# A two-stage conv network with four Fourier layers on one core: H transforms by even and odd halves, inverse W transform ahead of the second norm

## The reference, cut to what matters

```python
x = L0(x)                     # 3x3 conv, leaky relu, 1x1 conv to 9 weights, softmax, 9-tap filter per pixel
for j in range(4):            # x: 8 images, 32 channels, 64 x 64, float32
    Kj, Lj = project(K[j]), project(L[j])        # less the mean of the nine taps
    z = relu(batchnorm(conv3x3(x, Kj), gamma[j], beta[j]))      # conv1, first norm
    x = x + 0.1 * conv3x3T(z, Kj)                               # conv2
    x = batchnorm(x, gamma[j], beta[j])                         # second norm
    Bh = fft2(Lj, rolled and padded to 64 x 64)                 # one filter per channel
    t = 1.0 / (0.1 * (Bh.real ** 2 + Bh.imag ** 2) + 1.0)
    x = real(ifft2(fft2(x) * t))
```

## Time and profile before

| | |
|---|---|
| median of 3 runs | 695.11 us (694.95 to 696.44) |
| the profiled execution | 699.56 us, its span 697.7 us |
| TensorE (PE) busy | 643.2 us (92%) |
| VectorE (DVE) busy | 487.7 us (70%) |
| ScalarE (ACT) busy | 355.3 us (51%) |
| GpSimd (POOL) busy | 95.5 us (14%), all in the prologue |
| mean granted TensorE clock | 0.978 of full speed |

### The profile page before, as it was taken

One profiled execution on the slowest core, in us unless ns is written; L12 is line 12 of the kernel. 1 busy time (PEld: TensorE's weight loads), 2 busy tenths in 40 slices (PEclk: granted clock), 3 DMA queues, 4 the chain that ended last, 5 costly groups with the idle time before them and its releaser, 6 DMA issues.

```text
span 697.7 us, 13525 instructions
## 1 busy us (share of the span) xinstructions
PE 643.2 (92%) x5392; PEld 221.3 (32%) x5392; DVE 487.7 (70%) x843; ACT 355.3 (51%) x672; POOL 95.5 (14%) x92
## 2 busy tenths in 40 slices
PE   6597999999999989999999899999998999999982
PEld 4222333222333333233333332333333323333330
DVE  3669888875886794638867946398679453886783
ACT  1454666663796223528961325299523152994233
POOL 0367666672000000000000000000000000000000
PEclk9689999999999999999999999999999999999996
DMA  9995111115800013583000226730003177100044
GB/s 187 183 171 91 32 32 33 31 31 127 190 2 1 1 28 97 131 176 102 1 1 1 52 72 156 155 99 1 1 1 79 46 176 154 40 1 1 1 105 137
DMA packets 44781, 51.10 MB, mean 73 GB/s; under 512 B 36528, under 2 KB 36656, under 8 KB 42672
## 3 DMA queue, kind: packets, MB, share of 16 engines
q1 hardware_dynamic: 40240, 48.95, 32.9%
q10 hardware_dynamic: 4480, 1.30, 1.2%
HBM read 11.96 MB, written 4.19 MB: 23 GB/s over the span
## 4 chain that ended last, share of the span: by engine, by line
PE 77%; DVE 15%; issue 3%; ACT 2%; DMA 1%; SPq 1%; POOL 0%; DVEq 0%; ACTq 0%; POOLq 0%
PE psum L978 48%; PE psum L1050 6%; PE psum L1146 5%; PE psum L1113 5%; PE psum L1129 3%; PE psum L1160 3%; PE psum L1001 3%; DVE work L923 2%; PE psum L1038 2%; DVE spare L895 1%; DVE work L889 1%; ACT Z L614 1%; DVE work L905 1%; DVE work L879 1%; PE psum L1080 1%
## 5 line engine op out<-in xcount | busy, mean ns | idle before, releaser
L978 PE MATMUL psum<-Z,wts 128*32 128x512 f32 x1536 | 168.2, 593 | 6.4 <-DVE Z L846 6.4
L978 PE MATMUL psum<-X,wts 128*32 128x512 f32 x1536 | 170.1, 593 | 0.6 <-issue 0.6
L593 ACT ACTIVATE work<-X,small 128x512 bf16<-128x512 f32 x128 | 90.7, 710 | 48.6 <-DVE X L864 48.6
L768 DVE BATCH_NORM_STATS2 stats<-Z 128x6 f32<-128x512 f32 x60 | 41.3, 692 | 79.3 <-ACT Z L508 79.2
L508 ACT ACTIVATE Z<-psum 128x512 f32<-128x512 f32 x64 | 38.2, 597 | 104.3 <-PE psum L978 93.2
L978 PEld LDWEIGHTS psum<-Z,wts 128*32 128x32 f32 x1536 | 51.6, 109 | 121.5 <-issue 108.5
L978 PEld LDWEIGHTS psum<-X,wts 128*32 128x32 f32 x1536 | 47.9, 109 | 111.7 <-issue 110.7
L571 ACT ACTIVATE Z<-Z,small 128x512 f32<-128x512 f32 (+4 forms) x92 | 80.2, 922 | 5.2 <-DVE small L836 4.7
L864 DVE SCALAR_TENSOR_TENSOR X<-psum,X 128x512 f32<-128x512 f32 x64 | 43.6, 690 | 39.0 <-PE psum L978 38.8
L1146 PE MATMUL psum<-work,cstS 128*128 128x512 f32 x128 | 59.2, 605 | 4.7 <-DVE work L889 3.9
L1129 PE MATMUL psum<-work,cstS 128*128 128x496 f32 x128 | 56.3, 582 | 0.0
(11 more groups left out here) (122 smaller groups left out, 772.7 us busy)
## 6 DMA issues: line engine op xcount, KB each, us to landing
X<-X SPq DMA_DIRECT2D x64, 260.0 KB, 4.0
Z<-Z SPq DMA_DIRECT2D x32, 520.0 KB, 8.0
Z<-x SPq DMA_DIRECT2D x36, 128.0 KB, 4.2
out<-Z SPq DMA_DIRECT2D x24, 128.0 KB, 2.2
parS<-par SPq DMA_DIRECT2D x4, 673.0 KB, 8.6
Z<-x SPq DMA_DIRECT2D x12, 120.0 KB, 5.3
Z<-x ACTq DMA_DIRECT2D x14, 64.0 KB, 4.4
Z<-x SPq DMA_DIRECT2D x14, 64.0 KB, 4.7
```

Of the source, the lines that this page charges most:

```text
L593: nc.scalar.activation(by_row(rest[:, o:o + N // 2].bitcast(bf16)), xc, what, bias=small[:, 26:27], accum_out=sums[:, NCH * i + c:NCH * i ...
L768: nc.vector.bn_stats(stats[:, 6 * c:6 * c + 6], rows(Z0, REG, c // Q, CH * (c % Q), CH))
L978: last = nc.tensor.matmul(out_b[C * r:C * r + C, :], weights[:, o:o + C], rows(src, reg, bp, g, CH, dj - 1), start=(dj == 0), stop=(dj == ...
```

## The change

Four things are done together.

1. **H by halves.** GpSimd's `mix_halves` adds and subtracts image rows h and h + 32 of each pair, from X0 into Z0, as soon as conv2's chunks are there; `turn` reads Z0. The H transform of a sum gives the even and that of a difference the odd frequencies, so fwdH and invH become matmuls of 64 x 64 where there were 128 x 128. Two chunks together are four such matmuls on four quadrants of the array. `unmix_halves` adds and subtracts again after the inverse, from Z0 into X0. In the last layer invH stays a 128 x 128 matmul and gives the rows directly.
2. **Inverse along W ahead of the norm.** invW of pairs 0 and 1 runs before the second norm; `move_back` writes Z0, raw, and ScalarE's `scale_x` (step "affine") scales X0 in place, two operations of 1024 elements per pair (four of 512 before). In the last layer it writes Z2 from Z0.
3. **Order.** The transform steps stand one behind each chunk of conv2; fwdH of pair 3 moves behind conv1's chunk 1. `turn` of a pair stands behind the first conv2 chunk of the next pair, that of pair 3 behind the second norm and `prepare`.
4. Constants for the new matmuls; slot 0 takes seven small matmuls per pair, a table four (now three each, with half the columns or half the outputs).

```diff
     after = {
-        5: fourier(j, 0, "fwdW"),
-        9: fourier(j, 0, "fwdH") + fourier(j, 1, "fwdW"),
-        13: fourier(j, 0, "invH") + fourier(j, 1, "fwdH") + fourier(j, 2, "fwdW"),
-        15: fourier(j, 1, "invH") + fourier(j, 2, "fwdH"),
+        6: fourier(j, 0, "fwdW"),
+        8: fourier(j, 0, "fwdH"),
+        9: fourier(j, 1, "fwdW"),
+        10: fourier(j, 0, "invH"),
+        11: fourier(j, 1, "fwdH"),
+        12: fourier(j, 0, "invW"),
+        13: fourier(j, 2, "fwdW"),
+        14: fourier(j, 1, "invH"),
+        15: fourier(j, 2, "fwdH"),
     }
     for c in range(NCH):
-        steps += [("conv2", j, c), ("turn", j, c)] + after.get(c, [])
-    steps += [("norm", j, 2)] + fourier(j, 3, "fwdW") + fourier(j, 0, "invW") + fourier(j, 2, "invH")
-    steps += fourier(j, 1, "invW") + fourier(j, 3, "fwdH")
-    rest = {1: fourier(j, 3, "invH"), 3: fourier(j, 2, "invW"), 5: fourier(j, 3, "invW")}
+        steps.append(("conv2", j, c))
+        if c and c % Q == 0:
+            steps.append(("turn", j, c // Q - 1))
+        steps += after.get(c, [])
+    steps += [("moments", j)] + fourier(j, 1, "invW") + [("norm", j, 2), ("affine", j, 0), ("turn", j, BP - 1), ("affine", j, 1)]
+    steps += fourier(j, 3, "fwdW") + fourier(j, 2, "invH")
+    rest = {
+        1: fourier(j, 3, "fwdH"),
+        2: fourier(j, 2, "invW"),
+        3: fourier(j, 3, "invH"),
+        5: fourier(j, 3, "invW") + [("affine", j, 2)],
+        9: [("affine", j, 3)],
+    }
...
+            def mix_halves(j, bp, i):
+                bk.result(NUMBER["conv2", j, bp * Q + 2 + i])
+                low, high = (rows(X0, REG, bp, CH * (2 * half + i), CH) for half in range(2))
+                for half, op in enumerate((ALU.add, ALU.subtract)):
+                    nc.gpsimd.tensor_tensor(rows(Z0, REG, bp, CH * (2 * half + i), CH), low, high, op=op)\
+                        .then_inc(halves_mixed, 1)
+
+            def unmix_halves(j, bp):
+                pool.wait_ge(rows_back, 2 * (BP * j + bp) + 2)
+                pool.wait_ge(x_summed, 2 * (NCH * j + Q * bp + Q))
+                even, odd = (rows(Z0, REG, bp, 2 * CH * p, 2 * CH).rearrange("p g (b w) -> p g b w", b=2) for p in range(2))
+                for half, op in enumerate((ALU.add, ALU.subtract)):
+                    dst = rows(X0, REG, bp, 2 * CH * half, 2 * CH).rearrange("p g (w b) -> p g b w", b=2)
+                    nc.gpsimd.tensor_tensor(dst, even, odd, op=op).then_inc(parts_added, 1)
+
+            for j in range(DEPTH):
+                for what, *at in layer_steps(j):
+                    if what == "conv2" and at[1] % Q > 1:
+                        mix_halves(j, at[1] // Q, at[1] % Q - 2)
+                    elif what == "invW" and at[1] % Q == 0 and j + 1 < DEPTH:
+                        unmix_halves(j, at[1] // Q)
...
-            def keep_invW(j, c):
+            def scale_x(j, bp):
...
+                for h in range(2):
+                    if j == DEPTH - 1:
...
+                    else:
+                        act.wait_ge(parts_added, 2 * (BP * j + bp) + h + 1)
+                        dst = src = rows(X0, REG, bp, 2 * CH * h, 2 * CH)
+                    nc.scalar.activation(dst, src, ACT.Identity, bias=small[:, 13:14], scale=small[:, 12:13]).then_inc(x_back, 2)
...
                 for what, *at in layer_steps(j):
-                    if what == "norm" and at[1] == 1:
-                        scale_and_bias(j, 1)
-                        relu_first(j)
+                    if what == "norm":
+                        scale_and_bias(*at)
+                        if at[1] == 1:
+                            relu_first(j)
+                        elif j + 1 < DEPTH:
+                            dve.wait_ge(bn_ready, 2 * j + 2)
+                            prepare(j + 1)
+                            gamma_and_beta()
...
             def forward_h(j, c):
-                n, q = NUMBER["fwdH", j, c], c % Q
-                bk.claim(n)
-                nc.tensor.matmul(bank(n)[:, 0:16 * (SL - 1)], cm(C_FH),
-                                 freqw[:, N * q:N * q + N].rearrange("p (a s) -> p a s", s=SL)[:, :, 1:SL],
-                                 start=True, stop=True).then_inc(filled[n % BANKS], 1)
+                first, q = NUMBER["fwdH", j, c], c % Q
+                for x in range(2):
+                    bk.claim(first + x)
+                for x in range(2):
+                    for p in range(2):
+                        k, half = slice(64 * p, 64 * p + 64), 64 * (p ^ x)
+                        src = freqw[k, N * (q + x):N * (q + x) + N].rearrange("p (a s) -> p a s", s=SL)[:, :, 1:SL]
+                        last = nc.tensor.matmul(bank(first + x)[half:half + 64, 0:16 * (SL - 1)], cstS[k, C_FH:C_FH + 64], src,
+                                                start=True, stop=True, tile_position=(64 * p, half))
+                    last.then_inc(filled[(first + x) % BANKS], 1)
```

More of the change, by code:

```diff
@@ L35 @@
 PAIRS = NCH // 2
-C_FW, C_FH, C_IH, C_IL, C_IW, C_HH, C_HC, C_AVG, C_ERE, C_EIM = (128 * i for i in range(10))
+C_FW, C_IH, C_IL, C_IX, C_IW, C_HH, C_HC, C_AVG, C_ERE, C_EIM = (128 * i for i in range(10))
 C_CS = 10 * 128
@@ L153, in number_banks @@
     for step in steps:
-        if step in number or step[0] == "turn":
+        if step in number or step[0] in ("turn", "affine", "moments"):
             continue
@@ L632, in _ @@
                         keep_slot0(*at)
-                    elif what == "invW":
-                        keep_invW(*at)
+                    elif what == "affine":
+                        scale_x(*at)
                     elif what == "conv1":
@@ L869, in add_conv2, with turn @@
                     nc.vector.tensor_scalar(S(26), stats[:, 1:2], -1.0, None, ALU.mult).then_inc(shift_ready, 1)
[L871 to L876 removed]
+            def turn(j, bp, half):
+                dve.wait_ge(halves_mixed, Q * (BP * j + bp) + 3 + half)
+                k, g = 2 * bp + half, 2 * CH
+                o = bp * REG + g * GROUP * half
+                src = Z0[:, o + 2:o + 2 + g * GROUP].rearrange("p (g i) -> p g i", i=GROUP)[:, :, 0:ROW]
                 for b in range(2):
@@ L901, in move_back @@
                     bk.full(first + i)
-                k, b0 = 2 * bp + half, (first + 2 * half) % BANKS
-                if k > 2:
-                    dve.wait_ge(x_back, NCH * j + 2 * (k - 2))
-                nc.vector.transpose(turned[k % 3].rearrange("p (m e l) -> p e m l", e=2, l=32),
-                                    psum[:, b0:b0 + 2, :].rearrange("p e (c m) -> p e m c", c=C)).then_inc(rows_back, 1)
+                b0 = (first + 2 * half) % BANKS
+                for b in range(2):
+                    dst = rows(Z0, REG, bp, 2 * CH * half, 2 * CH).rearrange("p g (b e l) -> p b e g l", b=2, e=2)[:, b]
+                    src = psum[:, b0:b0 + 2, :].rearrange("p e (c g b) -> p b e g c", c=C, b=2)[:, b]
+                    last = nc.vector.transpose(dst, src)
+                last.then_inc(rows_back, 1)
             def scale_slot0(j, bp):
@@ L937, in _ @@
                     elif what == "turn":
-                        if at[1] % 2:
-                            turn(*at)
+                        for half in range(2):
+                            turn(*at, half)
                     elif what == "fwdW":
                         move_rows(*at)
-                        if at[1] == 3 * Q + 3 and j + 1 < DEPTH:
-                            dve.wait_ge(bn_ready, 2 * j + 2)
-                            prepare(j + 1)
-                            gamma_and_beta()
+                    elif what == "moments":
+                        aggregate_x(j)
                     elif what == "invH":
                         move_slots(*at)
-                        if at[1] == 2 * Q - 1:
-                            aggregate_x(j)
                     elif what == "invW" and at[1] % 2 == 0:
@@ L1136, in slot_0_back @@
                 bk.result(NUMBER["slot0", j, bp])
[L1137 to L1147 removed]
+                for x in range(2):
+                    for p in range(2):
+                        k = slice(64 * p, 64 * p + 64)
+                        last = nc.tensor.matmul(by_chunk(bank(n)[k, 0:2 * C], x), cstS[k, C_HC + 64 * x:C_HC + 64 * x + 64],
+                                                by_chunk(slot0[k], x), start=True, stop=True, tile_position=(64 * p, 64 * p))
+                last.then_inc(filled[n % BANKS], 1)
+            def inverse_h(j, c):
+                first, (bp, q) = NUMBER["invH", j, c], divmod(c, Q)
+                for x in range(2):
+                    bk.claim(first + x)
+                for x in range(2):
+                    bk.result(NUMBER["fwdH", j, c + x])
+                bk.result(NUMBER["slot0c", j, bp])
+                for x in range(2):
+                    src = spec[:, N * (q + x):N * (q + x) + N]
+                    if j == DEPTH - 1:
```

(6 more changed lines are left out.)

88 lines of the change are left out of this document (46 added, 42 removed).

## The result

The changed kernel takes **729.86 us**, median of 4 runs (728.25 to 730.13), beside 695.78 for the kernel before (694.95 to 697.32, 4 runs): a ratio of 1.048, interval 1.046 to 1.051, so 34.1 us slower. The prediction said 716.5 with a range up to 723: right in direction, too small by 13.4.

The account below looks back on a forecast made before the run. TensorE held 77% of the wait chain, with VectorE also at its limit in the turnover. Three full layers at +5.75 (+17.25) and the last at +4.2 gave +21.4: 721.0 profiled, less 4.45 offset, 716.5 us median; range 700 to 723.

Parts of the forecast that it names:

- the turnover: From conv2's end to conv1: 24.1 us forecast against 23.54 before, +0.55 per full layer.
- stretch 1: conv2 of each layer: waits for VectorE and ScalarE and a longer rest of conv2, +3.25 us per full layer.
- the last layer's tail: From the last layer's conv2 end to the kernel's end: 41.75 us forecast against 44.26, -2.5.
- stretch 3: conv1 with the remaining transforms: fwdH3 comes in, invH3 gets cheaper, a transfer wait is added; +1.95 us per full layer.
- VectorE's queue before turn 3: After conv2's end: VectorE's queued work lets turn 3 end only at 13.75 us, so TensorE stands over 9 us.
- the collision: Second norm: four VectorE operations with two SBUF inputs meet GpSimd's unmix, +3.8 us per full layer.
- the clock: TensorE's stop of 9 to 13 us halves its clock, so fwdW3 takes 3.8 us, not 1.9: +1.9.
- Rival B: Second norm: one-element-per-partition operations escape the GpSimd collision, 705 us (700 to 705 with smaller changes); chance 0.24.
- C: Transposes reading SBUF also collide with GpSimd, +1.5 us in each of four layers, 722.5 us; chance 0.1.
- D: Turnover short enough for TensorE: no collision, clock holds, ScalarE returns slot0c's bank in time; 690.5 us; chance 0.11.
- E: Only two array quadrants overlap, so fwdH and invH keep their price; some 735 us; chance 0.02.
- conv1 12: In conv1: this chunk waits for affine 3's transfer, 6.5 us after conv1 9 against 5.2; +1.3 (0 to 2).

Follow-up runs that it names:

- e1: Changed kernel with GpSimd's unmix of pair 1 held until prepare has made the new weights: 717.93 us, ratio 1.031.
- e4: Changed kernel with 13 unread filler matmuls (6 in the last layer) behind the norm's matmul, keeping TensorE busy: 719.19 us, ratio 1.033.
- e9_taps_later: Faster new order of the halves, with six fillers, changed further: taps prepared one conv1 chunk later, affine 3 behind conv1 7: 677.76 us, ratio 0.975.
- e12_fewer_fillers: Against e9_taps_later: moments, second norm ahead of fwdH2's scaling, norm's matmul ahead of invW1, four fillers instead of six: 678.61 us, ratio 0.974.
- e2: Changed kernel with turn 3 moved directly behind fwdH's scaling, ahead of the moments and second norm: 725.45 us, ratio 1.042.
- e3: Changed kernel with ScalarE doing keep_slot0 of pair 0 ahead of the sums of conv2 chunks 4 to 8: 725.48 us, ratio 1.041.
- e10_norm_sooner: Against e9_taps_later: moments, second norm ahead of fwdH2's scaling, norm's matmul ahead of invW1, nine fillers instead of six: 686.50 us, ratio 0.987.

## Why the prediction was right in direction and short in size

The mechanism stood: the three large prices of the turnover came out. The step that failed is **the adding up of the small terms, and the offset at its end**. The tables and anything special to the third layer were put at 0 and cost 2.6 and 2.8; stretch 1 was priced 0.75 too low in each of four layers; the gain of the last layer's tail was 1.0 too high; and 4.45 was taken off for an offset that was not there. The prologue, 2.3 shorter in this execution, is luck and hid as much of the miss. By the steps of the prediction, on the spans (+30.3 measured, +21.4 predicted):

| term of the sum | predicted | measured |
|---|---|---|
| prologue | 0 | -2.3 (within the spread of the variants) |
| tables, four times | 0 | +2.6 |
| stretch 1, per full layer | +3.25 | +4.0 |
| turnover, per full layer | +0.55 | +0.9 |
| stretch 3, per full layer | +1.95 | +2.2 |
| third layer besides | 0 | +2.8 |
| last layer to conv2's end, without its tables | +6.7 | +7.6 |
| its tail | -2.5 | -1.5 |

- **What held.** VectorE's queue before turn 3, the collision and the clock were each priced to within 0.2: fwdW3 ended 21.4 behind conv2's end (13.75 + 3.8 + 3.8 were walked), and e1 and e4 take the second and the third of these out at about their price (3.6 and 1.7 per layer, for 3.8 and 1.9). The turnover's miss lies behind fwdW3: from the start of invH2 to conv1 0 pass 3.03 where 2.55 was priced (and the terms as written add up to 24.0, not 24.1). The slow invH2 (2.63) is not the cause, for in e4 the same stretch took 3.03 with invH2 at 1.95; it is move_rows 3, with its start and its release. Rival B, that one-element operations slip past GpSimd, is refuted by L869 and e1. C is not borne out: in the kernel of `e9_taps_later` four transposes of turn 3 begun beside unmix took 2.54, beside 2.49 in the changed kernel, and 2.71 in `e12_fewer_fillers`, far from a loss of 1.2. D didn't come: neither the clock nor ScalarE's bank held. Nor did E: invH of a batch pair took 1.95, not 3.6.
- **PE work.** 13 us per full layer were to be freed; PE's busy time fell by 6.8. The packed matmuls were priced well (1.89 and 1.95 as read, for 1.75 and 1.9), but fragments, tables and the slow clock took back half.
- **The tables**, "0 to 0.3, hidden by the wait; I take 0". PE is busy 5.14 there instead of 3.98. Two of the tables stand ahead of the norm's matmul and made it 0.55 later (2.42 behind the first table instead of 1.87), so the wait moved with them and shrank only from 1.58 to 1.08: 0.65 each time, 2.6 in all. I took the wait for a fixed cover and did not look at what stands ahead of the instruction that it waits for.
- **Stretch 1.** Waits: 1.00, 1.50 and 1.22 measured, 1.3, 1.75 and 1.1 walked, good to 0.3. Most of the missing 0.75 is in what I priced as whole: spreading the steps makes convolutions single, 2.72 and not 2.65 each, and slot groups cost 0.6 and more with their switches. In four layers the miss is 3.
- **conv1 12**, "+1.3 (0 to 2)": 1.08, 1.00 and then 2.84. In the third layer the transfer landed 5.1 behind the end of its second issue instead of 3.3, and the four chunks behind the wait took 12.13 for 10.51. A window of the changed kernel over it shows why:

```profile
600.00:604.00 4.00, 3.65 (x20) 0.92 (x24) 0.00 (x0) 0.00 (x0) 0.00 (x0) 0.57 0.98 213
```

  The wait of 2.84 is followed by a mean clock of 0.57, so 1.2 GHz for most of it; behind the one of 1.08 it stayed at 1.00. The same late landing came in e1, e2 and e3 (waits of 2.69, 2.51 and 2.75), not in e4. Its cause stays open; that the wait itself need not exist is shown by e9.
- **The tail.** invH2 ran at the low clock there as well (4.65), and invW2 ended 25.5 behind conv2's end, where 24.35 was walked; the later steps kept about that distance.
- **The offset.** I took 4.45 off, since the profiled execution lay that much above the median. The one of after lay 0.2 above. It is no constant: profiled executions of the variants lie up to 2.5 below their medians and 1.6 above. So 4.2 of the 13.4 missed come from carrying it over. That it is chance fits the spread of the prologues, but what makes it stays open.
- **The range** reached to 723 by terms that I knew (C, 1.5 more in each layer). The terms left at 0 or priced too low came to about 11, all of one sign, and E, the next rival, lay at 735: the range should have had a bound for what the walk leaves out.

By the "GPSIMD Engine Reference" of the Trainium skill (Key points), GpSimd shares its SBUF interfaces with VectorE, with contention for instructions that have two SBUF inputs. By that rule, the trace agrees, down to a single element: 2.08 and 2.15 instead of 0.16 and 0.22, while the one-input L872 between them took 0.15. One input alone isn't a safe sign, though: L863 in `e10_norm_sooner` has one, of two elements, and took 0.72.

## What to carry to other kernels

Work taken off the busiest engine pays only with an order that keeps it fed: here packing was worth 10 us a layer and the rest of the change (order, collision, slow clock, tables) cost 18; another order for the same packing, with fillers, came out 19 us under the kernel before. Where a turnover ends in two chains (here turn, transform, move and norm, affine, transfer), write down both before moving a step; shortening one at the other's cost, as in e2 and e12, gives little or nothing. When an engine joins a chain (GpSimd between move_back and affine), price the chain and not only the engine. And when a sum has many small terms taken as 0, give their total a bound: fragments of work cost 0.05 to 0.1 a switch, a wait of 2.5 us cost the clock as well, and the offset of one execution is no constant.
